# A recurrent layer with four selectable cells: TensorE puts the input rows into the gate banks itself, and twelve steps of its code are written out

## What is computed

```python
g0 = x[:, 0] @ W_ih[0].T + b_ih[0] + b_hh[0]
h, c = _lstm_activate(g0, c0)                       # c0 = 0
def step(carry, x_t):
    h, c = carry
    sel_in = jnp.concatenate([h, c, x_t], axis=-1)
    logits = sel_in @ W_sel.T + b_sel
    onehot = jax.nn.one_hot(jnp.argmax(logits, axis=-1), Sx, dtype=x_t.dtype)
    g_all = einsum('bi,sgi->bsg', x_t, W_ih) + einsum('bh,sgh->bsg', h, W_hh) + b_ih + b_hh
    g = jnp.einsum('bsg,bs->bg', g_all, onehot)
    h2, c2 = _lstm_activate(g, c)   # sig(f)*c + sig(i)*tanh(g); sig(o)*tanh(c)
    return ((h2, c2), h2)
```

## Time and profile before

| | us |
|---|---|
| median of 3 runs | 6272.86 (6269.54 to 6273.96) |
| the profiled execution's own time | 6278.15 |
| its span in the profile | 6276.3 |
| mean granted TensorE clock over the span | 0.944 |

### The profile page before, as it was taken

How to read it: one execution, slowest core, us unless ns; L and a number is a source line. 1 busy time by engine, 2 the same in 40 slices (tenths; PEclk the granted TensorE clock), 3 DMA queues, 4 the chain that set the end, 5 groups by cost and what they waited for, 6 DMA issues and landing times. The chain is left out here.

```text
span 6276.3 us, 214043 instructions
## 1 busy us (share of the span) xinstructions
PE 5392.8 (86%) x84948; PEld 3269.5 (52%) x84948; DVE 3097.9 (49%) x13265; ACT 1088.6 (17%) x4645; POOL 612.9 (10%) x1014
## 2 busy tenths in 40 slices
PE   8998778849998929999999999999999999977778
PEld 6643443314666615555555555555555555544444
DVE  4401443214552165555555555555555555564543
ACT  0000000002331131111111111111111111122312
POOL 0000660002650000000000000000000000011100
PEclk9999998979999969999999999999999999989877
DMA  0000111467432330000000000000000000000010
GB/s 10 21 30 11 39 44 44 97 136 253 119 105 100 139 123 5 5 5 10 5 5 5 10 5 5 5 5 10 5 5 5 5 10 0 0 24 37 23 55 9
DMA packets 128787, 240.28 MB, mean 38 GB/s; under 512 B 47084, under 2 KB 64114, under 8 KB 127687
## 3 DMA queue, kind: packets, MB, share of 16 engines
q1 hardware_dynamic: 68584, 146.72, 6.6%
q0 software_dynamic: 60128, 92.58, 5.9%
HBM read 165.58 MB, written 73.29 MB: 38 GB/s over the span
## 5 line engine op out<-in xcount | busy, mean ns | idle before, releaser
L1456 PE MATMUL bank<-lstm_w,step_h_parts 128*32 128x128 f16 (+1 forms) x59904 | 1233.0, 238 | 172.1 <-issue 164.0
L1456 PEld LDWEIGHTS bank<-lstm_w,step_h_parts 128*32 128x32 f16 x59904 | 1116.8, 97 | 488.4 <-issue 478.0
L1427 PE MATMUL bank<-lstm_w 128*128 128x512 f16 x4992 | 1297.0, 383 | 3.2 <-issue 3.2
L1480 DVE TRANSPOSE_TENSOR_REDUCE step_summed<-bank 128x4 f32<-128x128 f32 x1872 | 670.0, 358 | 292.7 <-PE bank L1456 285.6
L1427 PEld LDWEIGHTS bank<-lstm_w 128*128 128x128 f16 x4992 | 386.4, 98 | 388.5 <-issue 5.1
L1406 ACT ACTIVATE step_act_out<-step_gates 128x4 f32<-128x4 f32 x625 | 128.5, 206 | 2082.3 <-DVE step_gates L1486 2078.8
L1486 DVE SCALAR_TENSOR_TENSOR step_gates<-step_summed,lstm_inv_scale,step_xgs 128x4 f32<-128x4 f32 x1872 | 416.0, 222 | 68.7
L1530 DVE COPY step_xgs<-step_xg 128x16 f32 x624 | 109.2, 175 | 688.7 <-issue 664.5
L1396 POOL COPY xnT<-step_state 128x4 f32 (+1 forms) x625 | 116.4, 186 | 3170.0 <-DVE step_state L1513 3170.0
L1109 PE MATMUL bank<-sum_parts,sum_hot 125*125 125x512 f16 x1600 | 347.6, 381 | 6.9 <-DVE sum_parts L1068 6.9
L1437 PE MATMUL bank<-lstm_wsel,step_state 128*1 128x4 f32 x4992 | 214.9, 168 | 115.3 <-DVE step_state L1503 115.3
(11 more groups left out here) (368 smaller groups left out, 6578.2 us busy)
## 6 DMA issues: line engine op xcount, KB each, us to landing
rel_h<-rel_h_sb SPq DMA_DIRECT2D x39, 1024.0 KB, 4.3
lstm_xg<-xg_g POOLq DMA_DIRECT2D x4, 5000.0 KB, 19.5
step_xg<-lstm_xg SPq DMA_DIRECT2D x25, 800.0 KB, 4.4
xg_w<-in_c_w_ih SPq DMA_DIRECT2D x8, 2048.0 KB, 10.7
lstm_w<-in_c_w_hh SPq DMA_DIRECT2D x4, 4096.0 KB, 30.8
rel_z<-rel_z_sb POOLq DMA_DIRECT2D x8, 1250.0 KB, 22.9
rel_zg<-rel_z POOLq DMA_DIRECT2D x8, 1248.0 KB
cheb_w<-in_L_gnn_weight SPq DMA_DIRECT2D x8, 1024.0 KB
```

The source lines that it names most:

```text
L1427: nc.tensor.matmul(idle[:], w[:, 0, 0, 0, 0, 0:128], w[:, 0, 0, 0, 0, :], start=True, stop=True)
L1456: last = nc.tensor.matmul(bank[32 * q:32 * q + 32, 0:32 * (end - first)], h_parts[:, c, :], w[:, s, c, q, a, 32 * first:32 * end], start=( ...
L1480: nc.vector.tensor_reduce(summed[:, first:end], bank[:, 0:32 * (end - first)].rearrange("p (b r) -> p b r", r=32), X_AXIS, ALU.add, apply_ ...
```

## The change

*Inputs.* `lstm_inputs` now puts steps on partitions and gates in columns: 16 groups (cell-gate pairs by position) x 5 tiles of 125 steps, each of 4 products of 512 columns. Each result is split into three bfloat16 parts by ScalarE and DVE in turn, and GpSimd's queue stores each tile, 80 stores of 384 KB. The biases are split the same way and stored once.

*Steps.* `xg` holds, for 12 steps and the first, 48 rows of input parts and 48 rows of bias parts. A product with a constant 0/1 matrix times the weights' scale (`rows`) places the rows of all four cells of a gate into that gate's bank, one quarter of the columns for each cell: four products of 128x512 (`inject`) between the score and the pick. The chosen cell then adds its products to its quarter, now for four gates in four banks, 4 x 32 products of 128 columns. DVE reduces the chosen quarter by a register address; ScalarE takes the sum with the scale. `xgs`, `gates` and `add_input` go. The dummy products go, all eight of a step.

*Loops.* PE's loop runs 52 times over 12 steps written out, each with all four cells: the ring's slot is then a constant in the code. DVE's loop begins with `choose` and ends with `finish`.

The diff, cut to its core (`split_weights` also keeps `L.up`, the scale times H_SCALE; the host lays W_ih and the biases out by gate and makes `c_xg_rows`):

```diff
+GATES = 4
+XG_CHUNK = 4
+XG_SLOTS = 3
+XG_RING = XG_SLOTS * XG_CHUNK
+XG_ROWS = GATES * 4 * 3
...
+            for i in range(TILES):
+                n, m = i // NT, i % NT
+                pool.wait_ge(lo_ready, i + 1)
+                pool.dma_start(B.xg[n, :, m * R:(m + 1) * R, :].rearrange("a t g -> t a g"), parts[:, i % 4]
+                               ).then_inc(stored[i % 4], 16)
+            for k in range(4):
+                pool.wait_ge(stored[k], 16 * (TILES // 4))
...
+            def take_rest(i):
+                if i >= 4:
+                    dve.wait_ge(lo_ready, i - 3)
+                dve.wait_ge(hi_ready, i + 1)
+                nc.vector.tensor_tensor(rest[:, i % 4], B.bank[i % 6][0:R, :], parts[:, i % 4, 0], ALU.subtract
+                                        ).then_inc(rest_ready, 1)
+
+            def take_lo(i):
+                dve.wait_ge(mid_ready, i + 1)
+                nc.vector.tensor_tensor(parts[:, i % 4, 2], rest[:, i % 4], parts[:, i % 4, 1], ALU.subtract
+                                        ).then_inc(lo_ready, 1)
...
+            def keep_hi(i):
+                if i >= 4:
+                    act.wait_ge(stored[i % 4], 16 * (i // 4))
+                act.wait_ge(done, i + 1)
+                nc.scalar.copy(parts[:, i % 4, 0], B.bank[i % 6][0:R, :]).then_inc(hi_ready, 1)
+
+            def keep_mid(i):
+                act.wait_ge(rest_ready, i + 1)
+                nc.scalar.copy(parts[:, i % 4, 1], rest[:, i % 4]).then_inc(mid_ready, 1)
...
+                if i >= 6:
+                    pe.wait_ge(rest_ready, i - 5)
...
+                    last = nc.tensor.matmul(B.bank[i % 6][0:R, :], xnT[:, c, m * R:(m + 1) * R], w[:, n % 2, c, :],
...
+            def load(k, slot):
+                sp.dma_start(xg[0:XG_ROWS, slot * XG_CHUNK:(slot + 1) * XG_CHUNK, :],
+                             xg_rows[:, bass.ds(k * XG_CHUNK + 1, XG_CHUNK), :]).then_inc(xg_loaded[slot], 16)
+
+            sp.dma_start(rows_f[:], I["c_xg_rows"]).then_inc(rows_loaded, 16)
+            sp.wait_ge(cleared, 1)
+            sp.dma_start(xg[0:XG_ROWS, XG_RING:XG_RING + 1, :], xg_rows[:, 0:1, :]).then_inc(first_loaded, 16)
+            sp.dma_start(xg[64:64 + XG_ROWS, :, :], bias_rows.to_broadcast((XG_ROWS, XG_RING + 1, 512))
+                         ).then_inc(first_loaded, 16)
+            for slot in range(XG_SLOTS):
+                load(slot, slot)
+            with sp.Fori(1, ROUNDS) as r:
+                for slot in range(XG_SLOTS):
+                    sp.wait_ge(init, 1)
+                    sp.wait_ge(injected, (r * XG_SLOTS + slot - (XG_SLOTS - 1)) * XG_CHUNK)
+                    load(r * XG_SLOTS + slot, slot)
...
+                act.wait_ge(summed_f, n)
+                nc.scalar.activation(act_out[:, 0:4], summed[:, 0:4], ACT.Sigmoid, scale=L.inv[:, 0:1]
+                                     ).then_inc(sig_f, 1)
...
-            def keep_clock_up(products):
-
-                for _ in range(products):
-                    nc.tensor.matmul(idle[:], w[:, 0, 0, 0, 0, 0:128], w[:, 0, 0, 0, 0, :], start=True, stop=True)
-
-            pe.wait_ge(init, 1)
-            with pe.Fori(1, STEPS) as t:
-
-                pe.wait_ge(init, 1)
-                pe.wait_ge(input_score_ready, t)
+            def inject(part, at, stop):
+                p, bank, _, _ = part
+                return nc.tensor.matmul(bank[:], rows[:, p, :], xg[:, at, :], start=True, stop=stop)
+
+            def add_half(part, s, c, a, stop):
+                p, bank, _, _ = part
+                for q in range(4):
+                    last = nc.tensor.matmul(bank[32 * q:32 * q + 32, 128 * s:128 * s + 128], h_parts[:, c, :],
+                                            w[:, s, c, q, a, 128 * p:128 * p + 128], start=False, stop=stop,
+                                            tile_position=(0, 32 * q))
+                return last
+
+            def cell(s):
+                for part in parts:
+                    for c, a in halves:
+                        last = add_half(part, s, c, a, stop=(c == KC - 1 and a == 1))
+                    last.then_inc(part[2], 1)
+
+            def step(t, at):
+
+                if at % XG_CHUNK == 0:
+                    pe.wait_ge(xg_loaded[at // XG_CHUNK], 16)
+                    pe.sem_inc(xg_loaded[at // XG_CHUNK], -16)
+                pe.wait_ge(input_score_ready, 1)
+                pe.sem_inc(input_score_ready, -1)
                 nc.tensor.matmul(score[:, 0:CELLS], B.ones[0:1, 0:1], input_score[:], start=True, stop=False)
                 pe.wait_ge(c_ready, t)
                 for k in range(KC):
@@ -1441,25 +1500,13 @@
                     last = nc.tensor.matmul(score[:, 0:CELLS], tc[:, k:k + 1], h_weight[:, :, k], start=False,
                                             stop=(k == KC - 1))
                 last.then_inc(score_done, 1)
-                keep_clock_up(WARM_PICK - 1)
-                pe.wait_ge(init, 1)
+                for part in parts:
+                    pe.wait_ge(part[3], t)
+                    last = inject(part, at, stop=False)
+                last.then_inc(injected, 1)
+                pe.wait_ge(picked, 1)
                 pe.wait_ge(h_lo_ready, t)
-                keep_clock_up(1)
-                pe.wait_ge(picked, 1)
                 s = pe.value_load(pick[0:1, 0:1])
-
-                def cell(s):
-                    for first, end, bank, done, _, _ in parts:
-                        for c in range(KC):
-                            for a in range(2):
-                                for q in range(4):
-                                    last = nc.tensor.matmul(
-                                        bank[32 * q:32 * q + 32, 0:32 * (end - first)], h_parts[:, c, :],
-                                        w[:, s, c, q, a, 32 * first:32 * end],
-                                        start=(c == 0 and a == 0), stop=(c == KC - 1 and a == 1),
-                                        tile_position=(0, 32 * q))
-                        last.then_inc(done, 1)
-
                 with pe.If(s < 2):
                     with pe.If(s < 1):
                         cell(0)
@@ -1470,22 +1517,23 @@
                         cell(2)
                     with pe.Else():
                         cell(3)
-                keep_clock_up(WARM_GATES)
+
+            pe.wait_ge(init, 1)
+            pe.wait_ge(rows_ready, 1)
+            pe.wait_ge(first_loaded, 32)
+            for part in parts:
+                inject(part, XG_RING, stop=True).then_inc(part[2], 1)
+            with pe.Fori(0, ROUNDS) as r:
+                for at in range(XG_RING):
+                    step(pe.snap(r * XG_RING + (at + 1)), at)
...
-            def add_input(part, t):
-                first, end, _, _, summed_part, gates_part = part
-                dve.wait_ge(summed_part, t)
-                nc.vector.scalar_tensor_tensor(out=gates[:, first:end], in0=summed[:, first:end],
-                                               scalar=L.inv[:, 0:1], in1=xgs[:, first:end], op0=ALU.mult,
-                                               op1=ALU.add).then_inc(gates_part, 1)
+            def add_rows(part, s, n):
+                p, bank, done, summed_part = part
+                nc.vector.tensor_reduce(summed[:, 4 * p:4 * p + 4], bank[:, bass.ds(s * 128, 128)].rearrange(
+                    "p (b r) -> p b r", r=32), X_AXIS, ALU.add, apply_transpose=True
+                                        )._wait_ge(done, 1).then_inc(summed_part, 1)
...
+            def parts_taken():
+                dve.sem_inc(done_f, -1)
+                dve.sem_inc(done_g, -1)
+                dve.sem_inc(done_i, -1)
+                dve.sem_inc(done_o, -1)
+
             def choose(t):
 
                 dve.wait_ge(score_done, 1)
@@ -1526,47 +1578,39 @@
                 nc.vector.max_index(pick[:], top[:], score).then_inc(picked, 1)
                 dve.wait_ge(picked, 1)
                 s = dve.value_load(pick[0:1, 0:1], min_val=0, max_val=CELLS - 1)
-                dve.wait_ge(xg_loaded, (t // CHUNK + 1) * 16)
-                nc.vector.tensor_copy(xgs[:], xg[:, bass.ds(s, 1), bass.ds((t % RING) * GC, GC)]
-                                      ).then_inc(xgs_ready, 1)
                 dve.sem_inc(score_done, -1)
                 dve.sem_inc(top_ready, -1)
-
-            def finish(t, n):
-
-                add_rows(part_f, t)
-                dve.sem_inc(picked, -1)
-                dve.wait_ge(xgs_ready, t)
-                add_input(part_f, t)
-                add_rows(part_ig, t)
+                parts_taken()
+                return s
+
+            def finish(s, t, n):
+
+                add_rows(part_f, s, n)
+                if t is not None:
+                    dve.sem_inc(picked, -1)
+                add_rows(part_g, s, n)
                 forget(n)
-                add_input(part_ig, t)
-                add_rows(part_o, t)
+                add_rows(part_i, s, n)
```

(61 more changed lines are left out.)

171 lines of the change are left out of this document (70 added, 101 removed).

## The result

The changed kernel takes 10,876.08 us (median of 4 runs, 10,874.51 to 10,886.19) for 6271.50 of the kernel before in the same measurements: a ratio of 1.7345, 95% interval 1.7315 to 1.7375. The prediction said 10,000 us, from 7,400 to 12,800.

What follows compares the result with a forecast made beforehand. One chain across engines bounds each 5.17 us step; written out, PE would wait for code blocks. Waits, boundaries and clock give 11.2 us a step: plus 3760, plus 10 for the start, said as 10,000 us, range 7,400 to 12,800.

Steps and rivals of the forecast that it cites:

- Rival 1: PE's code is never late, so only the other parts count: 6,160 to 6,230 us, faster; chance 0.13.
- rival 4: Without dummies and fetch waits PE falls to 1.2 GHz, lengthening cell and injects: 7,650 us; chance 0.03.
- rival 2: Blocks come further ahead, hiding boundaries in cells but not one long jump a step: 8,050 us; chance 0.18.
- Rival 3: A jump must bring all blocks between, 15.6 us a step: 12,800 us; chance 0.10.
- Entries for cell 3: PE's way to cell 3: one jump into a new block, 3.65 us; step with this cell 11.05 us.
- The clock: PE's loop: at 1.2 GHz cell work not covered by fetches takes 0.8 longer in part of the steps, plus 0.2 us.
- the waits inside the cells: Each 256-instruction cell always crosses a block boundary; the next block is usable some 3.65 us after being asked for.
- The packets: Instruction queue in PE's loop: two to three packets a step, some 1,700 in all.
- The gates' tail: From the cell's products to c: copy and three DVE additions go, minus 0.5 us a step, bounds minus 0.3 to 0.6.
- DVE's loop branch: Moves from behind the pick to between h_lo and MAX8, onto the path: about 0.3 us a step, bounds 0.1 to 0.4.
- injecting: Four 128x512 products replace four dummies of 1.04 us in the pick's time: nothing more at the full clock.
- The start and the input stage: Start of steps plus 10 us, bounds 5 to 20; input stage 0, bounds minus 15 to plus 30.

Runs made afterwards that it cites:

- the loops of 1,690 and 2,180 instructions: Two steps written out in PE's loop: in the kernel before (1,690 instructions) 6276.00 us, in the changed kernel (2,180 instructions) 11,332.77 us.
- the kernel without jumps: Changed kernel, twelve steps written out, each running cell 0 alone with no branch at the cells: 6622.41 us, ratio 1.0554.
- the first experiment: Changed kernel with one step in PE's loop instead of twelve (a ring of one slot), all else as changed: 6361.62 us, ratio 1.0131.
- the fastest kernel: Changed kernel with one step in PE's loop, three dummy products behind the cell and DVE's loop written out for four steps: 6040.71 us, ratio 0.9628.

## Why the prediction was right, and where its sum was short

**The mechanism held.** Code comes in blocks that stay only while the loop is small, one block ahead, at 3.2 to 4.0 us on average for a jump that finds nothing on its way or has only just asked for it: shown by removing the writing out (minus 4514 us), by adding it alone to the kernel before (plus 4078 us), by the loops of 1,690 and 2,180 instructions on either side of the store's size, and by the kernel without jumps. Rival 1 (code never late) and rival 4 (the clock alone) fell with the first experiment, rival 2 (blocks further ahead) with the pauses of the kernel without jumps. Rival 3 (a jump brings all blocks between) falls with the branches of the kernel after. On average the jump out of cell 0, over three cells, takes 3.75 us, the one out of cell 1, over two, 3.95, the outer branch over two 3.61, the inner one over cell 2 alone 3.24, and during each of the 322 outer ones a single packet started. The two other jumps over a single cell are shorter, into cell 1 1.74 us and out of cell 2 2.35. That fits a block already asked for when the jump begins.

**The sum gave 11.2 us a step, and 12.5 came.** Three of its terms were too small:
- *Entries for cell 3.* I counted one new block on the way to it, and put cell 3 (11.05) ahead of cells 1 and 2. The two nested branches land twice, and cell 3 is the longest, 15.14, so that the order is 0 < 1 < 2 < 3 and not the 0 < 3 < 1 < 2 forecast. The way to the cell is 7.34 us for 4.15 of cell 2: 3.2 us x 129 / 624 = 0.66 us a step.
- *The clock.* I took 0.2 us a step. A cell's products without their pauses take 4.28 - 1.30 = 2.98 us for 1.91: 1.07 us a step, 670 us in all. With no waits for code and no dummies either, the loop's clock was 0.95 (the first experiment), so it is the waits that took it down to 0.58.
- *The loop's branch.* I left it out; 4.7 us in one step of twelve is 0.39.

Together they are 0.66 + 0.87 + 0.39 = 1.9, and only 1.3 came, so other terms were 0.6 too large. By cells: clock and loop branch should add some 1.4 to 1.5 us to each period of the sum, and cell 0 came out 1.8 longer (9.96 for 8.2), cell 1 0.7 (12.59 for 11.85), cell 2 0.3 (13.23 for 12.95). What I counted too high are the waits inside the cells, and the trace of the kernel after shows how. In 381 of the 428 steps with cells 1 to 3 the cell has a pause. The first product behind it starts 3.3, 3.15 and 3.3 us (cells 1, 2 and 3) after the branch into the cell has ended, where I took 3.65. It comes no later at the half clock: in cell 2 after 3.2 us in the steps at the half clock and 3.1 in those above it, in cell 3 after 3.3 and 3.4, with a pause of 2.0 to 2.1 us in the first and 1.5 to 1.6 in the second. So products slowed ahead of a pause cost nothing, and the 1.07 us above count them. How the 0.6 divides between the two wasn't worked out. That the whole came out within 9% of 10,000 owes something to these errors of opposite sign.

**The packets.** I expected 1,700, one for each entry; 2380 came. The excess fits the blocks asked ahead and then jumped over: ahead of the step with cell 3 shown above a packet starts at 5010.36, the outer branch at 5010.81 jumps past it, and the packet for its landing starts at 5011.88. It was not tested by itself.

**The other parts.** The gates' tail: c is written 2.45 us after the cell's first product (4013.27 to 4015.72 in the fastest kernel) for 3.03 before: minus 0.58, expected minus 0.5. DVE's loop branch: 0.39, expected 0.3, bounds 0.1 to 0.4. The net, in steps at the full clock, is 5.04 for 5.16: minus 0.12 where I had minus 0.2. That injecting costs nothing at the full clock held: the four take 1.04 us, in the pick's time, as the dummies did. That the dummies could go for nothing didn't: 140 us in the kernel with one step. The start and the input stage: plus 32 us where I had plus 10, inside the bounds. In the input stage ScalarE waits 206.7 us for the stores, which land 9.1 us after their issue at the median and have four buffers; whether more buffers would help was not tested. The waits (who for whom, us in total, times, longest):

```profile
POOL lstm_xg L1184 <- DVE xg_parts L1200: 257.3, 70, 57.1
ACT xg_parts L1230 <- DMA lstm_xg<-xg_parts: 206.7, 66, 10.2
```

## What to carry to other kernels

Count a loop's instructions before writing out its body. On PE a loop of 1,690 stayed and one of 2,180 was fetched again in each pass, and where such a loop branched over its alternatives each landing in another block cost 1.7 to 4.0 us on average, by how long before its block had been asked for. With the branches at the cells gone the loss was 0.4 to 0.6 us a step, with the jump back and the clock in it. The first pass of the loop before showed the price beforehand: look there for a branch with a maximum far over its median, and for packets of the instruction queue. And ask of a loop's own branch what stands behind it: moved from behind the pick to ahead of MAX8, DVE's cost 0.39 us in every step.

## What the runs showed of the hardware that was not expected

- Just over the size that stays is worse than far over it: 13.24 us a step with two steps written out, 12.49 with twelve. The loop's branch, 4.6 us, comes six times as often, 1.9 us more a step, of which 0.75 is left in the whole; where the rest is made good wasn't worked out.
- Eight dummy products a step did not hold the clock once PE waited for its code: 0.73 over the span of the kernel before with twelve steps, 0.94 without.
- The clock depends on small differences in what PE does: without dummies 92 steps met the half clock where a step took 5.28 us on average, 46 where it took 4.86, and with three dummies 2.
- A jump back to the start of a loop that doesn't stay is dear even where the loop has no other branch: 4.55 us at the median, 52 times.
- ScalarE's activations with the scale read from SBUF take 297 ns for 206 without.
